# A graph kernel: the table of group places moved to a multiple of 16 bytes

## The reference, cut to what matters

```python
h = relu(layernorm(x));  x = x + two_layers(h)      # each: rrelu(norm * segment_sum((e_h + h[src]) @ W_r, dst) + self_msg)
h = relu(layernorm(x));  x = x + attention(h)       # softmax over the edges that end in a node, then Wo and a layer norm
```

## Time and profile before

| | us |
|---|---|
| three runs | 788.82, 790.39, 792.11 |
| median | 790.39 |
| the profiled execution | 794.31 |
| its span, first to last instruction | 792.6 |
| PE busy in the span | 720.0 (91%) |
| DVE busy in the span | 518.6 (65%) |
| ACT busy in the span | 432.6 (55%) |

### The profile page before, as it was taken

One profiled execution on the slowest core, in us unless ns is written; L12 is line 12 of the kernel. 1 busy time (PEld: TensorE's weight loads), 2 busy tenths in 40 slices (PEclk: granted clock), 3 DMA queues, 4 the chain that ended last, 5 costly groups with the idle time before them and its releaser, 6 DMA issues.

```text
span 792.6 us, 15463 instructions
## 1 busy us (share of the span) xinstructions
PE 720.0 (91%) x5799; PEld 533.1 (67%) x5799; DVE 518.6 (65%) x928; ACT 432.6 (55%) x1088; POOL 247.1 (31%) x274
## 2 busy tenths in 40 slices
PE   4665699989899999999999999799999999999996
PEld 3554588879789999888899999344444444444455
DVE  5998999968788877552333343335574757666676
ACT  1566666646566656662221121467676767767663
POOL 7220010000000222210000000256675766667675
PEclk9999999989999999999999999889999999999999
DMA  4112000133310000012222111210010000000010
GB/s 134 45 26 58 1 2 8 31 103 66 101 32 9 8 9 9 30 44 64 75 90 68 40 35 40 91 32 1 1 26 1 18 8 14 13 14 13 1 26 20
DMA packets 39763, 27.89 MB, mean 35 GB/s; under 512 B 5311, under 2 KB 38288, under 8 KB 39686
## 3 DMA queue, kind: packets, MB, share of 16 engines
q1 hardware_dynamic: 38514, 25.89, 11.2%
q10 hardware_dynamic: 1172, 0.98, 0.4%
HBM read 13.28 MB, written 10.80 MB: 30 GB/s over the span
## 4 chain that ended last, share of the span: by engine, by line
PE 74%; DVE 8%; issue 6%; ACT 6%; DMA 2%; POOL 2%; ACTq 1%; POOLq 0%; DVEq 0%; SPq 0%
PE sums L1539 16%; PE sums L1522 15%; PE sums L1035 12%; PE sums L1108 12%; PE sums L1074 8%; DVE work L860 3%; DVE work L854 2%; DMA x_after_messages<-work 2%; ACT counts L1310 2%; PE sums L1042 1%; PE sums L1136 1%; PE sums L1049 1%; PE sums L1115 1%; POOL counts L668 1%; POOL counts L696 1%
## 5 line engine op out<-in xcount | busy, mean ns | idle before, releaser
L1618 POOL TENSOR_TENSOR counts<-counts,work 125x500 f32<-125x500 f32 x150 | 165.0, 1100 | 99.9 <-DVE work L1688 94.6
L1688 DVE SCALAR_TENSOR_TENSOR work<-sums,counts 125x500 f32<-125x500 f32 x150 | 101.6, 677 | 106.1 <-ACT sums L1642 100.8
L1074 PE MATMUL sums<-work 125*128 125x196 f16 (+15 forms) x1220 | 153.7, 252 | 14.0 <-DVE work L860 14.0
L1539 PE MATMUL sums<-work 125*128 125x500 f32 (+1 forms) x350 | 159.7, 546 | 6.8 <-DVE work L1688 6.2
L1522 PE MATMUL sums<-work 128*125 128x500 f32 x300 | 152.2, 589 | 0.0
L1637 ACT ACTIVATE sums<-sums,steady 125x500 f32<-125x500 f32 (+1 forms) x157 | 102.3, 652 | 74.9 <-PE sums L1522 71.7
L854 DVE TENSOR_TENSOR work<-work,counts 125x3024 f16<-125x3024 f16 (+1 forms) x60 | 114.4, 1906 | 41.1 <-PE sums L1076 40.2
L1310 ACT CAST counts<-sums 128x364 f32 (+38 forms) x305 | 132.1, 474 | 2.6 <-issue 0.8
L1076 PE MATMUL sums<-work 125*128 125x10 f16 (+15 forms) x800 | 130.0, 193 | 0.0
L860 DVE TENSOR_TENSOR work<-work,counts 125x4200 f16<-125x4200 f16 (+15 forms) x120 | 125.5, 1087 | 0.0
L1035 PE MATMUL sums<-counts 125*128 125x250 f16 (+1 forms) x975 | 121.8, 269 | 4.0 <-ACT work L1240 3.8
(11 more groups left out here) (181 smaller groups left out, 657.9 us busy)
## 6 DMA issues: line engine op xcount, KB each, us to landing
first_columns<-counts SPq DMA_DIRECT2D x5, 610.4 KB
counts<-first_columns SPq DMA_DIRECT2D x5, 610.4 KB
counts<-counts SPq DMA_DIRECT2D x5, 468.8 KB
counts<-in_x SPq DMA_DIRECT2D x5, 312.5 KB
h_nodes<-counts SPq DMA_DIRECT2D x5, 312.5 KB
work<-in_x SPq DMA_DIRECT2D x12, 125.0 KB
x_after_messages<-work SPq DMA_DIRECT2D x12, 125.0 KB
h_attention<-work SPq DMA_DIRECT2D x12, 125.0 KB
```

Source lines behind the costliest of these rows:

```text
L1074: pe.matmul(win[:, 0:c, cols], lo[:, k * 2 * LO:k * 2 * LO + 128], m[:, k, h0 * w:(h0 + c) * w].rearrange("p (h d) -> p h d", d=w), start= ...
L1539: last = pe.matmul(ps_o[c % 2][:, 0:cols(u) // n], h3[:, source(c, j + i), :], pbuf[u % PB][:, i * NP:i * NP + cols(u) // n], start=j + i ...
L1618: pool.tensor_tensor(a, a, p, ALU.add).then_inc(acc_done, 1)
L1688: dve.scalar_tensor_tensor(pbuf[u % PB], ps_s[u % 4][0:NP, 0:WIDE], float(np.exp(-CLIP)), counts[0:NP, source(c, j), target(c) * WIDE:(tar ...
```

## The change

A line is put ahead of the placing of `places`, which rounds its first byte up to a multiple of 16. That moves `places` from byte 41260 to 41264 of `work`, and the three small tiles behind it (`ones_h`, `degs`, `half`) by the same 4 bytes. All tiles that come later in the function begin at places of their own. No instruction is added, taken out or moved. [...]

```diff
@@ -191,6 +191,8 @@
     place("t2", NP, LB * D)
     place("iota_h", NP, NB * WM + WM % 2, F16)
     place("carry", 128, 2 * 28, F16)
+
+    at += -at % 16
     place("places", 1, GROUPS, I32)
     place("ones_h", RL, 2, F16)
     place("degs", NP, NB)
```

## The result

Over the rounds on the chip the changed kernel took 780.0 us (778.79 to 781.16, six runs) and the kernel before 791.25 us (788.82 to 793.38, six runs). The ratio is 0.9859, with a 95% interval of 0.9834 to 0.9884: 11 us faster, against a forecast of 778 with a range of 770 to 790. The profiled execution took 780.53 us with a span of 778.8, where the one of before had 794.31 and 792.6.

What follows compares the result with a forecast made beforehand. VectorE's one-hots were taken as the bound up to about 158 us, TensorE after that. Gains of 2.7 + 5.7 + 4.6 + 1.5 = 14.5 us took 794.3 to 779.8, then 778 for the median, range 770 to 790.

Steps and rivals of the forecast that it cites:

- the low end: Load at L1280: between 0.91 us (no change) and 0.29 us (single access), 0.35 us was taken, near the one-word load.
- second rival: Load at L1280 stays at 0.91 us, word after word whatever the line; nothing moves, 790.4 us; chance 0.13.
- the excess paid by each access: Disturbed loads wait behind DMA traffic at each access; 4.11 us over four is 1.03 each, so the longest takes 1.38 us.
- first rival: Only the load's fixed part shrinks, one wait per DMA burst: 5.02 becomes 4.46 us, 4.7 gained, 785.7 us; chance 0.12.
- My bound that no load exceeds 2 us: Sign to look for at L1280: a median near 350 ns and a longest load below 2 us.
- the cover of some 2.3 us: Past 160 us, the load time PE can take without a pause at the carry matmul: some 2.3 us.
- (a): Up to 158 us, VectorE's waits for the ring behind three long early loads go: 2.7 us gained.
- (b): Past 158 us, PE's pauses of 3.25, 1.84 and 0.63 us at the carry matmul go: 5.7 us gained.
- (c): Half-clock stretches behind the pauses of 3.25 and 1.84 us go, half of PE's busy time there: 4.6 us gained.
- (d): At ends of chunks, PE's waits for ScalarE's copies where a load stands in the way shrink: 1.5 us gained.
- From the profile to the median: Half of the 3.9 us by which the profiled execution stood above the median was taken off: 779.8 to 778 us.
- slower rival: One wide access waits longer in DMA traffic than four narrow ones; one or two further long loads give 797 us; chance 0.07.

Runs made afterwards that it cites:

- the two kernels with the second table: Loads of groups 108 to 143 read another table: kernel before, table on a multiple of 16, 783.2 us; changed kernel, table 12 past, 789.7 us.
- the two stops: Changed kernel with ScalarE made to wait for a chain of GpSimd operations, at group 108 (786.7 us) or at group 176 (783.5 us).
- the two of 2.37 us: TensorE pauses behind group 108's load in two kernels with `places` 8 and 4 past a multiple of 16; single runs of 789.6 and 789.4 us.
- the stop at 108: Changed kernel with ScalarE made to wait at group 108 for a chain of five small GpSimd operations: 786.7 us, ratio 0.9948 to the kernel before.

## Why the prediction was right

**The load.** Taken at 0.35 us between 0.91 and 0.29, it is 0.31. The choice of the low end was right, though no row of before separated it from the other: it was my guess. That off a multiple of 16 four words take the time of word after word is what all three places show (0.91 us), but two words within one line do so as well (0.49). The 206 ns a word of the second rival fit each further word here (0.29, 0.49, 0.91 us for one, two and four) and fail for the four on a multiple of 16 (0.31). That rival, which went by a fixed price for each word, is out.

**The disturbed loads.** For the longest load, that of group 108, the excess paid by each access gave 1.38 us for 5.02, and 1.07 came out. The first rival, in which only the fixed part shrinks, would have had 4.46; the two kernels with the second table speak against it at the same group. As a mechanism the excess by access is not shown, though. Over the quiet 0.91 and 0.31 us the seven long loads had 16.2 us before and have 5.5 now, a third and not a quarter; that of group 136 has lost none of it (1.98 us before, 2.07 now), as by the rival, and loads of two words took up to 3.58 us, an excess of 3.1 where two accesses of 1.03 would make 2.1. My bound that no load exceeds 2 us was too tight: group 136 has 2.38 us, and it leaves PE a pause of 0.11 us, which fits the cover of some 2.3 us. That so long a load cost nothing here was luck in part: it ends at the edge of that cover.

**(a) 2.7 us up to 158 us.** The profiles have 3.1 at group 36 and 3.0 at group 108, with the three waits of VectorE gone.

**(b) and (c), pauses of 5.7 and half clock of 4.6 us.** Together 10.3; from group 108 to 144 the profiles have 68.5 and 58.2 us, 10.3. The clock stays at 1.00 there. The halving in (c) follows the granted 0.50, and the matmuls bear it out: six of L1035 in 1.26 us behind the pause, in 0.65 ahead of it. How large each part is, the two stops show by themselves. That both longer pauses of before had a half clock behind them the prediction read from their own rows; that a pause brings it each time would have been wrong, as the two of 2.37 us show.

**(d) 1.5 us at the ends of chunks.** This term was mis-sized. From group 36 to 108 the gain doesn't grow (3.1 and 3.0 us), and from group 144 to 196 the profiles have 106.2 and 105.9 us, 0.3. Of the waits in the earlier trace rows the first stands as it was, and only the last is shorter:

```profile
123.69 0.70 PE L1057 MATMUL sums<-work 128*125 128x128 f32 x4 [0.58 <-ACT work L1259]
...
310.91 1.77 PE L1037 MATMUL sums<-counts 125*128 125x250 f16 x15 [0.44 <-ACT work L1242]
```

A load stood near the first of them, not in the way. Before, the load of group 84 ran from 125.4 to 126.3 us, while ScalarE worked without a gap from 125.1 to 126.5 us on instructions issued ahead of it, of which the copy that PE waits for (L1257) is the last. The load was hidden behind them, and I had not followed the chain back at each place.

**From the profile to the median.** 2.7 + 5.7 + 4.6 + 1.5 gave 779.8 for a profiled execution, which took 780.5. I took off 2 us more, half of the 3.9 by which the profiled execution of before stood over its median. The changed kernel's profiled run and its median lie within 0.5 us of each other (780.5, 780.0), so for this kernel only 0.5 was to come off: the profiles differ by 13.8 us and the medians by 11.2. The 780.0 measured is 2.0 above the forecast, within the stated range. One reason is in sight. The long loads off the multiple vary: in the five profiled kernels that have loads of four words off it there, with the transfers in their old place, group 108 to 144 took 64.3 and 66.9 us (table 4 and 8 past), 68.5 (before), 70.1 (the second table 12 past) and 71.5 (only the tiles behind moved), against 58.1 to 58.3 in the four whose loads there lie on the multiple and meet no added stop. So part of the gain read from one profile need not be there in the usual run. That this is what sets the profiled execution of before above its median is not shown; no run here shows the loads of an execution without the profiler.

**The slower rival**, longer waits of a wide access in traffic, is out: each of the 50 loads of the changed kernel is shorter than that of the same group before.

## What to carry to other kernels

When a sequencer reads several words into registers, look at the byte at which they begin: here four int32 from a multiple of 16 took 0.31 us and from any other place tried 0.91, and two at a time 0.49 each. Look at the longest of such loads and not at their median: one small stop of the engine that hands over the carry could be paid twice, as TensorE's pause (4.94 us with the stop at 108) and as a half clock behind it (some 3.0 us more), and nine of 50 loads made most of the gain. Before a wait is counted as a gain, follow it back: a load that stands near a wait need not be what it waits for.

## What was not expected of the hardware

A register load off the multiple of 16 took 5.02 us under DMA traffic of 103 GB/s (group 108 before, 156.5 to 161.6 us), over five times the median of 0.91, while five others, in traffic of 82 GB/s on average (163 to 198 us), took 0.91 to 1.11 us.

A granted clock of 1.00 in a row need not be a reading. In the profiled run with the stop at 108 the granted clock is 0.50 from 9 to 94 us:

```profile
9.00:94.00 85.00, 54.21 (x636) 47.68 (x637) 81.60 (x149) 48.73 (x169) 20.22 (x28) 0.50 0.17 45
```

The same stretch of the changed kernel says 1.00:

```profile
9.00:94.00 85.00, 54.11 (x636) 47.59 (x637) 80.99 (x148) 48.65 (x169) 20.19 (x29) 1.00 0.16 44
```

Yet PE took the same 54 us for the same 636 matmuls. The matmuls themselves tell which row to believe. Those of L1076 with 175 columns in the changed kernel, from 95 to 99.3 and from 99.5 to 103 us (count, ns least/median/most):

```profile
L1076 PE MATMUL sums<-work x12: 328/329/348, 95.6 to 98.8; 125*128 125x175 f16 x12
...
L1076 PE MATMUL sums<-work x16: 246/247/257, 99.9 to 102.7; 125*128 125x175 f16 x16
```

The kernel with the stop at 108 has 328 ns for the same shape where its row says 0.50, and 256 ns from 95 us, where it says 1.00. In the changed kernel the step from 329 to 247 ns comes between 98.8 and 99.9 us, and its trace holds no clock record before 99.3 us: its 1.00 up to there stands for a missing record. So both ran the stretch from 9 to 94 us with the matmul times that go with a granted clock of 0.50 where there are records. The same holds for the kernel before, whose records begin at 89.2 us: its matmuls with 150 columns took 328 ns up to 89 us and 247 from there on, so the 1.00 from 27 to 60 us in the earlier trace rows is no reading either. The sum of the prediction doesn't use it. In the stretch of the long loads, past 150 us, all the traces have records, and the time of the matmuls agrees with them: in the kernel before, those of L1035 with 250 columns took 415 ns at 0.50 (205.4 to 208.5 us) and 270 at most from 208.8 us on, at 1.00. Whether the lower clock costs anything in the early stretch, where VectorE is busy 81 of 85 us, stays open: no kernel here ran the whole of it at 1.00, as in every trace matmuls with 150 columns still took up to 329 or 330 ns from 84 to 88 us.
